# GNN layer pair on one Trainium2 core: the edge loop's accumulators filled by ScalarE, its bias folded into a constant, its attributes scaled before they are turned, and the second LayerNorm's moments taken another way

## The chip, the cores and the metric

One Trainium2 chip, one NeuronCore of it. The metric is the device time of one execution in microseconds (us): the median of three runs of the kernel before is 1620.67 us (1620.6 to 1627.65).

## What is computed

There are N = 50,000 nodes with 128 features and E = 25,000 edges sorted by their receiver `dst`. Cut to what matters:

```python
h = maximum(layernorm(x), 0)
# layer 0, on edges (src, dst):
m = concat([h[dst], h[src]]) @ W_pre.T + b_pre
agg = concat([max, min, mean, std of m over the edges of a node])
scaled = concat([agg, agg * log(deg + 1), agg / log(deg + 1)])
x = x + (concat([h, scaled]) @ W_post.T + b_post) @ W_lin.T + b_lin
h = maximum(layernorm(x), 0)
# layer 1:
mean_attr = segment_mean(edge_attr, dst)
x = x + relu(concat([h, mean_attr]) @ W1 + b1) @ W2 + b2
```

## The kernel before

**Two passes.** The node pass treats every node as if it had no edge, in 98 chunks of 512 nodes. It writes the output rows `y` and a `table` that holds, for every node, its first normalised row and its `x`. The edge pass goes over the edges in 49 chunks of 512 edges (4 tiles of 128). It gathers the sender's and the receiver's rows from `table`, and scatters finished rows over those of the node pass for nodes that have edges. Chunk by chunk each engine runs its own hand-written program; `run_passes` calls `node_step` and then `edge_step` on each of them, and semaphores tie the programs together.

**One edge step.** In step k the engines work on several chunks at once, each in the order that its `edge_step` spells out:

- GpSimd (POOL) gathers the rows of chunk k+4: eight indirect DMAs in `gather`, for four tiles two each. Between them `receiver_const` adds a constant to the receivers' x of chunk k+1 into `xdc`. Then come the four indirect DMAs of `scatter` for chunk k-2, and `mean_attr`, which multiplies the running sum of the attributes by 1/count into `attr_mean` for chunk k.
- TensorE (PE) turns the sender's rows (`turn_sender`) and the receiver's (`turn_receiver`) of chunk k+1, makes the sender's part of the message (`sender_part`), and does the heavy part, `layer0`, in four tiles of chunk k: max, min and mean of the messages, each split into a high and a low part, the deviation and the receiver's row against the combined weights, added up in banks 5 and 6 in turn. For chunk k-1 it turns the second normalised rows (`turn_normed`), computes `hidden` from them and from `attr_mean`, and `outputs`, where one matmul of ones (L701) puts the bias b2 into bank 7 and sixteen add the product.
- ScalarE (ACT) moves turned rows out of PSUM, adds the bias b_pre to the message (`message`), squares it, makes high parts, normalises chunk k-1, and takes roots.
- VectorE (DVE) runs five scans over the 512 edges of a chunk (max, min, sum, sum of squares, attributes) that restart at every new receiver, makes low parts, and for each tile of `layer0` runs `mix`: three operations that scale and add the three 128-column blocks, giving x after layer 0. `moments` takes mean and variance of that from four bn_stats and four bn_aggr. `factors` turns them into scale and shift.
- SyncE (SP) loads masks for chunk k+4 (four rows, broadcast to all partitions) and attributes for chunk k+2.

The gathered rows lie in four buffers, `attr_mean`, `xdc`, `x1` and most others in two. Before a tile of `layer0`, PE waits until `mix` has read that bank (L605); `hidden` waits for POOL's product:

```python
pe.wait_ge(sem("e_attr_mean"), c + 1 + EU * i)
```

The order of PE in a step is turn_sender(k+1), layer0(k,0), sender_part(k+1), turn_receiver(k+1), layer0(k,1), turn_normed(k-1), layer0(k,2), turn_attr(k), hidden(k-1), layer0(k,3), outputs(k-1) (L708 to L730).

## Time and profile before

| | |
|---|---|
| median of three runs | 1620.67 us (1620.6 to 1627.65) |
| the profiled execution, its own time | 1626.46 us |
| its span, first to last instruction | 1624.7 us |
| granted TensorE clock, mean | 0.973 |
| node pass, about | 0 to 560 us |
| edge pass, about | 560 us to the end |
| busy: PE, DVE, POOL, ACT | 1494.9, 1397.1, 1236.0, 939.8 us |
| DMA moved | 197.95 MB, mean 122 GB/s |

A busy engine is one that has an instruction running; an engine's idle time is put down to what ended it. "Issue" stands for time in which nothing that the profile shows was waited for. PE's granted clock is 1.00 at 2.4 GHz and 0.50 at 1.2 GHz. A step of the edge pass is most easily read off a line that runs once per chunk.

### The profile page before, as it was taken

To read this page: it belongs to the slowest core of one execution; us is meant where nothing else is said; L and a number is where in the kernel's file an instruction comes from. 1 tells how busy PE (TensorE), PEld (TensorE's weight loads), DVE (VectorE), ACT (ScalarE), POOL (GpSimd) and SP (SyncE) were. 2 spreads that over 40 slices of the span, in tenths; PEclk is the share of its full clock that TensorE was granted. 3 is DMA by queue.
4 is the path that set the end of the run, shared out by engine and by line. 5 is a ranking of instruction groups with operands and counts; after the bars stand their busy time and mean duration, and the time that the engine had idled before them with its cause. 6 is when DMAs were issued, how large, how long until landed. Compare 5 with 4: busy or idle time off the path is not lost.

```text
span 1624.7 us, 33700 instructions
## 1 busy us (share of the span) xinstructions
PE 1494.9 (92%) x8747; PEld 1257.4 (77%) x8747; DVE 1397.1 (86%) x4327; ACT 939.8 (58%) x1976; POOL 1236.0 (76%) x1376
## 2 busy tenths in 40 slices
PE   2899999999999759999999999999998999999995
PEld 2799998889999648888777787777777777777783
DVE  5899999999999468899888997988887888888892
ACT  1799999999999534455444453434444444444341
POOL 1778777777778777888888888888888888888833
PEclk9899999999999979999999999999999999999997
DMA  3455555555555622233233333333332323333200
GB/s 88 163 209 206 207 207 201 201 201 204 204 203 206 187 87 85 84 86 90 90 91 92 93 92 91 92 91 89 93 91 79 95 86 89 94 93 93 89 18 15
DMA packets 158898, 197.95 MB, mean 122 GB/s; under 512 B 18912, under 2 KB 115321, under 8 KB 158858
## 3 DMA queue, kind: packets, MB, share of 16 engines
q1 hardware_dynamic: 136906, 149.93, 28.3%
q0 software_dynamic: 21952, 47.55, 9.5%
q8 instruction: 17, 0.28, 0.1%
q14 instruction: 23, 0.19, 0.0%
HBM read 111.11 MB, written 90.17 MB: 124 GB/s over the span
## 4 chain that ended last, share of the span: by engine, by line
PE 82%; DVE 6%; issue 5%; ACT 3%; another core or an unknown queue 3%; DMA 1%; SPq 1%; POOL 0%; DVEq 0%; ACTq 0%; POOLq 0%
PE bank L572 12%; PE bank L621 6%; PE bank L581 6%; PE bank L614 5%; PE bank L691 5%; PE bank L618 5%; PE bank L615 5%; PE bank L624 5%; PE bank L704 5%; PE bank L670 3%; PE bank L593 3%; PE bank L591 3%; PE bank L592 3%; PE bank L555 3%
## 5 line engine op out<-in xcount | busy, mean ns | idle before, releaser
L444 POOL DMA_INDIRECT rows<-table,idx x196 | 208.3, 1063 | 59.7 <-issue 59.7
L450 POOL DMA_INDIRECT y<-nout,oidx x196 | 200.0, 1020 | 70.6 <-issue 70.3
L444 POOL DMA_INDIRECT hs<-table,idx x196 | 204.8, 1045 | 44.7 <-issue 31.2
L614 PE MATMUL bank<-comb_lo,agg_hi 128*128 128x384 f32 x588 | 212.4, 361 | 16.6 <-DVE nout L1019 10.7
L572 PE MATMUL bank<-w_sb,nut 128*128 128x128 f32 x1568 | 202.9, 283 | 5.5 <-issue 4.7
L379 POOL TENSOR_TENSOR runs<-nx,b_all 128x512 f32<-128x512 f32 x98 | 125.9, 1284 | 107.9 <-DVE nx L1029 107.8
L572 PEld LDWEIGHTS bank<-w_sb,nut 128*128 128x128 f32 x1568 | 184.5, 193 | 23.1 <-issue 14.2
L618 PE MATMUL bank<-comb_hi,agg_lo 128*128 128x384 f32 x588 | 200.1, 340 | 0.0
L615 PE MATMUL bank<-comb_hi,agg_hi 128*128 128x384 f32 x588 | 199.5, 339 | 0.0
L781 ACT ACTIVATE nh<-nx,nms,nrs 128x128 f32<-128x128 f32 x392 | 161.8, 484 | 1.1 <-DVE nms L1002 0.5
L621 PE MATMUL bank<-comb_sd,agg_sd 128*128 128x384 f32 x392 | 159.6, 489 | 0.0
L865 ACT ACTIVATE nut<-bank,b_col 128x512 f32<-128x512 f32 x98 | 67.5, 689 | 151.9 <-PE bank L696 138.4
L391 POOL TENSOR_SCALAR rows<-rows,nmv,nrs 128x128 f32<-128x128 f32 x196 | 154.6, 798 | 0.0
L388 POOL TENSOR_TENSOR xdc<-rows,lone_const 128x512 f32<-128x512 f32 x98 | 125.1, 1276 | 32.7 <-DVE nrs L1039 32.7
L691 PE MATMUL bank<-attr_mean,w_attr 128*128 128x512 f32 x196 | 111.3, 652 | 30.9 <-issue 30.2
L796 ACT ACTIVATE nut<-bank,b_col 128x512 f32<-128x512 f32 x196 | 125.6, 681 | 15.3 <-remote 11.2
L1100 DVE SCALAR_TENSOR_TENSOR part<-bank,amp_att,xdc 128x128 f32<-128x128 f32 x196 | 67.6, 345 | 75.8 <-remote 27.1
L614 PEld LDWEIGHTS bank<-comb_lo,agg_hi 128*128 128x128 f32 x588 | 111.3, 189 | 20.5 <-issue 14.8
L624 PE MATMUL bank<-comb_h_lo,hdt 128*128 128x384 f32 x196 | 125.0, 638 | 0.0
L810 ACT ACTIVATE hst<-bank 128x512 f32<-128x512 f32 x49 | 29.3, 598 | 164.2 <-PE bank L637 130.5
L615 PEld LDWEIGHTS bank<-comb_hi,agg_hi 128*128 128x128 f32 x588 | 111.6, 190 | 2.2
L618 PEld LDWEIGHTS bank<-comb_hi,agg_lo 128*128 128x128 f32 x588 | 111.1, 189 | 0.0
(180 smaller groups left out, 4196.9 us busy)
## 6 DMA issues: line engine op xcount, KB each, us to landing
table<-rows SPq DMA_DIRECT2D x98, 512.0 KB, 2.7
rows<-in_x SPq DMA_DIRECT2D x98, 256.0 KB, 3.1
y<-nout SPq DMA_DIRECT2D x98, 256.0 KB
inv<-inv_row SPq DMA_DIRECT2D x49, 256.0 KB
attr<-in_edge_attr SPq DMA_DIRECT2D x48, 256.0 KB
keep<-keep_row SPq DMA_DIRECT2D x49, 128.0 KB
reset<-reset_row SPq DMA_DIRECT2D x49, 128.0 KB
lift<-lift_row SPq DMA_DIRECT2D x49, 128.0 KB
```

What stands on the lines that cost most here:

```text
L379: pool.tensor_tensor(nx1b[:, c % 4], nx1[:, c % 2], b2_all[:], ALU.add).then_inc(sem("n_x1b"), 1)
L391: last = pool.tensor_scalar(nh[:, c % 4, j, :], nx[:, c % 4, j, :], nmv1[:, c % 4, j, 0:1], nrs1[:, c % 4, j:j + 1], ALU.subtract, ALU.mult)
L444: pool.indirect_dma_start(out=to[:, s, j, :], out_offset=None, in_=of, in_offset=bass.IndirectOffsetOnAxis(ap=idx[:, s, which, j:j + 1], a ...
L450: pool.indirect_dma_start(out=out, out_offset=bass.IndirectOffsetOnAxis(ap=oidx[:, c % 4, j:j + 1], axis=0), in_=eout[:, c % 2, j, :], in_ ...
L572: mm = pe.matmul(bank[5][:, j * P:(j + 1) * P], nut[:, c % 2, m, j * P:(j + 1) * P], w2_sb[:, m, :], start=(m == 0), stop=(m == 1))
L614: pe.matmul(acc[:, 0:SCALERS * P], hi, w_lo, start=(a == MX), stop=False, skip_group_check=True)
L615: pe.matmul(acc[:, 0:SCALERS * P], hi, w_hi, start=False, stop=False, skip_group_check=True)
L618: pe.matmul(acc[:, 0:SCALERS * P], lo, w_hi, start=False, stop=False, skip_group_check=True)
L621: pe.matmul(acc[:, 0:SCALERS * P], agg_sd[:, c % 2, cols], comb_sd[:].rearrange("p s f -> p (s f)"), start=False, stop=False, skip_group_c ...
L624: mm = pe.matmul(acc[:, 0:SCALERS * P], h[:, c % 2, cols], w[:].rearrange("p s f -> p (s f)"), start=False, stop=(w is comb_h_hi and h is ...
L691: pe.matmul(bank[b][:], w1_attr[:, cols], attr_mean[:, c % 2, :], start=True, stop=False)
L781: last = act.activation(nh2[:, b, j, :], nx1[:, b, j, :], ACT.Identity, scale=nrs2[:, b, j:j + 1], bias=nms2[:, b, j:j + 1])
```

## The change

- **Fills.** ScalarE's new `seed` copies a constant of 384 columns (`acc_seed`) into bank 5 or 6 ahead of every tile of `layer0`; the matmuls add to it, and PE now waits for `e_seeded`. The constant holds b_lin and b_post (which `edge_const` added to the receivers' x before) and what b_pre contributes. `out_bias` copies b2 into bank 7, in place of the matmul of ones. POOL's `receiver_const` goes; `mix` reads the gathered x itself.
- **Bias as a constant.** `message` goes: the scans read the banks 3 and 4, in which `sender_part` now writes in turn, and the square is taken without bias.
- **Attributes scaled, then turned.** ScalarE's `scale_attr` multiplies the rows of attributes by 1/count before PE turns them, and the scan uses a new fp32 mask `keepm` = (count-1)/count, so its result is the mean already. POOL's `mean_attr` goes. `keepm` is one more broadcast row for SP, 256 KB per chunk.
- **Moments.** The third operation of `mix` also puts out the sum of its 128 columns (`accum_out`), `negative_mean` scales it, and ScalarE's `squares` puts out the sum of squares of x minus its mean.
- **Order.** PE's `turn_attr`, `turn_receiver` and `sender_part` move ahead of `layer0(k,0)`; DVE's scans are set in another order; gathers run three chunks ahead and not four, since their buffer is now free only when `mix` has read it.

The diff, cut to its core:

```diff
@@ inputs and setup
+    keepm_row = nc.dram_tensor("keepm_row", [ROWS * RW], F32, kind="Internal").ap()
-    edge_const = sb("edge_const", [P, TILES, P])
+    edge_const = sb("edge_const", [P, P])
+    acc_seed = sb("acc_seed", [P, SCALERS * P])
+    b_pre_wide = sb("b_pre_wide", [P, P])
-    attr_mean = sb("attr_mean", [P, 2, CHUNK])
+    keepm = sb("keepm", [P, 4, CHUNK])
...
+            dve.scalar_tensor_tensor(keepm_sb[R], count[R], -1.0, inv_count[R], ALU.add, ALU.mult).then_inc(sem("masks_done"), 1)
...
+            dve.tensor_tensor(acc_seed[:, 0:P], bank[6][:, P:2 * P], edge_const[:], ALU.add)
+            dve.tensor_copy(acc_seed[:, P:SCALERS * P], bank[6][:, 2 * P:(1 + SCALERS) * P]).then_inc(sem("seed_ready"), 1)
@@ SyncE, edge_step
-                        sp.wait_ge(sem("e_attr_mean"), c - 3 + EU * i)
+                        sp.wait_ge(sem("e_max"), c - 3 + EU * i)
...
+                        sp.wait_ge(sem("e_attr_run"), c - 3 + EU * i)
...
-                    for dst_sb, row in ((keep, keep_row), (reset, reset_row), (lift, lift_row), (inv, inv_row)):
+                    for dst_sb, row in ((keep, keep_row), (reset, reset_row), (lift, lift_row), (inv, inv_row),
+                                        (keepm, keepm_row)):
@@ GpSimd
-            def receiver_const(c, i):
...
-                pool.tensor_tensor(xdc[:, c % 2], xd[:, c % 4], edge_const[:], ALU.add).then_inc(sem("e_xdc"), 1)
...
-                    pool.wait_ge(sem("e_xdc"), c - 3 + EU * i)
+                    pool.wait_ge(sem("e_mixed"), TILES * (c - 3) + TILES * EU * i)
...
-            def mean_attr(c, i):
...
-                pool.tensor_tensor(attr_mean[:, c % 2, :], run_attr[:, c % 2, :], inv[:, c % 4, :],
-                                   ALU.mult).then_inc(sem("e_attr_mean"), 1)
...
             def edge_step(k, i):
-                if edge(k + 1):
-                    copy_scales(k + 1, i)
-                if edge(k + 4):
-                    gather_rows_of(k + 4, i)
-                    pool.wait_ge(sem("e_idx"), k + 5 + EU * i)
-                    go()
-                    gather(k + 4, (0, 1))
-                if edge(k + 1):
-                    receiver_const(k + 1, i)
-                if edge(k + 4):
-                    if edge(k + 1):
-                        pool.wait_ge(sem("e_xdc"), k + 2 + EU * i)
-                        go()
-                    gather(k + 4, (2, 3))
+                if edge(k + 3):
+                    gather_rows_of(k + 3, i)
+                    pool.wait_ge(sem("e_idx"), k + 4 + EU * i)
+                    go(0)
+                    gather(k + 3, (0, 1))
+                if edge(k + 2):
+                    copy_factors(k + 2, i)
+                if edge(k + 3):
+                    if edge(k + 2):
+                        pool.wait_ge(sem("e_factors"), k + 3 + EU * i)
+                        go(1)
+                    gather(k + 3, (2, 3))
                 if edge(k - 2):
...
                     scatter(k - 2)
-                if edge(k):
-                    mean_attr(k, i)
@@ TensorE
             def layer0(c, j, i):
                 acc = bank[5 + j % 2]
...
-                if j >= 2:
-                    pe.wait_ge(sem("e_mixed"), TILES * c + j - 1 + TILES * EU * i)
...
+                pe.wait_ge(sem("e_seeded"), TILES * c + j + 1 + TILES * EU * i)
...
-                    pe.matmul(acc[:, 0:SCALERS * P], hi, w_lo, start=(a == MX), stop=False, skip_group_check=True)
+                    pe.matmul(acc[:, 0:SCALERS * P], hi, w_lo, start=False, stop=False, skip_group_check=True)
...
             def sender_part(c, i):
                 pe.wait_ge(sem("e_hst"), c + 1 + EU * i)
...
-                pe.matmul(bank[3][:], ws_t[:], hst[:, c % 2, :], start=True, stop=True).then_inc(sem("e_b_psum"), 1)
+                pe.matmul(bank[3 + c % 2][:], ws_t[:], hst[:, c % 2, :], start=True, stop=True).then_inc(sem("e_b_psum"), 1)
...
-                    pe.matmul(bank[b][:], w1_attr[:, cols], attr_mean[:, c % 2, :], start=True, stop=False)
+                pe.matmul(bank[b][:], w1_attr[:, cols], run_attr[:, c % 2, :], start=True, stop=False)
...
             def outputs(c, i):
                 pe.wait_ge(sem("e_ut"), 2 * (c + 1) + 2 * EU * i)
-                pe.matmul(bank[7][:], ones[:], b2_rows[:], start=True, stop=False, skip_group_check=True)
+                pe.wait_ge(sem("e_b2"), c + 1 + EU * i)
@@ ScalarE
+            def squares(c, i):
...
+                for j in range(TILES):
+                    last = act.activation(off2[:, j, :], x1[:, b, j, :], ACT.Square, bias=neg2[:, b, j:j + 1],
+                                          accum_out=sq2[:, b, j:j + 1])
...
-            def message(c, i):
...
-                act.activation(bank[4][:], bank[3][:], ACT.Identity, bias=b_pre_col[:]).then_inc(sem("e_b"), 1)
...
-                act.activation(bsq[:, c % 2, :], bank[3][:], ACT.Square, bias=b_pre_col[:]).then_inc(sem("e_bsq"), 1)
+                act.activation(bsq[:, c % 2, :], bank[3 + c % 2][:], ACT.Square).then_inc(sem("e_bsq"), 1)
...
+            def seed(c, j, i):
...
+                act.activation(bank[5 + j % 2][:, 0:SCALERS * P], acc_seed[:], ACT.Copy).then_inc(sem("e_seeded"), 1)
+
+            def scale_attr(c, i):
...
+                for j in range(TILES):
+                    last = act.activation(attr[:, c % 2, j, :], attr[:, c % 2, j, :], ACT.Copy,
+                                          scale=factor[:, c % 4, 2, j:j + 1])
...
+            def out_bias(c, i):
...
+                act.activation(bank[7][:], b2_all[:].rearrange("p j f -> p (j f)"), ACT.Copy).then_inc(sem("e_b2"), 1)
@@ VectorE
-                dve.tensor_tensor(x1[:, c % 2, j, :], acc[:, 0:P], part2[:, j % 2, :], ALU.add).then_inc(sem("e_mixed"), 1)
+                dve.scalar_tensor_tensor(x1[:, c % 2, j, :], acc[:, 0:P], 1.0, part2[:, j % 2, :], ALU.mult, ALU.add,
+                                         accum_out=sum2[:, c % 2, j:j + 1]).then_inc(sem("e_mixed"), 1)
...
-                dve.tensor_tensor_scan(run_attr[:, b, :], keep[:, s, :], bank[2][:], run_attr[:, 1 - b, end] if c else 0.0,
+                dve.tensor_tensor_scan(run_attr[:, b, :], keepm[:, s, :], bank[2][:], run_attr[:, 1 - b, end] if c else 0.0,
...
-            def moments(c, i):
...
-                for j in range(TILES):
-                    last = dve.bn_stats(bn2[:, b, j, :], x1[:, b, j, :])
...
+            def negative_mean(c, i):
...
+                dve.tensor_scalar(neg2[:, b, :], sum2[:, b, :], -1.0 / P, None, ALU.mult).then_inc(sem("e_neg2"), 1)
...
             def edge_step(k, i):
...
                 if edge(k - 2):
                     outputs(k - 2, i)
+                if have:
+                    scan_attr(k, i)
+                if ahead:
+                    scan_min(k + 1, i)
                 if behind:
                     factors(k - 1, i)
                 if have:
                     mix(k, 0, i)
                 if ahead:
+                    receiver_low(k + 1, i)
                     scan_max(k + 1, i)
-                    scan_min(k + 1, i)
-                    scan_sum(k + 1, i)
-                    message_mean(k + 1, i)
-                    receiver_low(k + 1, i)
...
```

What moves on an engine, as the lists of each engine's instructions in program order have it. ScalarE first, one whole step of the edge pass of the kernel before (line, operation, output<-inputs, shape):

```order
L810 ACTIVATE hst<-bank 128x512
L802 ACTIVATE sd<-mv,eps_col 128x4
L835 ACTIVATE bank<-bank,b_pre_col 128x512
L816 ACTIVATE hdt<-bank 128x512
L824 ACTIVATE nh<-nx,ms,rs 128x128 x4
L841 ACTIVATE bsq<-bank,b_pre_col 128x512
L847 ACTIVATE nh2t<-bank 128x512
L853 ACTIVATE agg_hi<-runs 128x512 x2
L859 ACTIVATE mean_b<-mean_b 128x512
L853 ACTIVATE agg_hi<-mean_b 128x512
L865 ACTIVATE nut<-bank,b_col 128x512 x2
L869 ACTIVATE var<-var 128x512
```

and the first twelve rows of the same step with the change; eight rows follow to the step's end, among them one more fill of a tile (L875) and the fill of bank 7 (L888):

```order
L820 ACTIVATE hst<-bank 128x512
L804 ACTIVATE off,sq<-nx,neg 128x128 x4
L842 ACTIVATE bsq<-bank 128x512
L875 ACTIVATE bank<-acc_seed 128x384
L812 ACTIVATE sd<-sq,eps_col 128x4
L826 ACTIVATE hdt<-bank 128x512
L834 ACTIVATE nh<-nx,ms,rs 128x128 x4
L875 ACTIVATE bank<-acc_seed 128x384
L854 ACTIVATE agg_hi<-runs 128x512
L848 ACTIVATE nh2t<-bank 128x512
L882 ACTIVATE attr<-attr,factor 128x128 x4
L875 ACTIVATE bank<-acc_seed 128x384
```

The four squares (L804), whose input DVE finishes last in the step before, now stand ahead of the squared message (L842) and of the fill of tile 1 (L875). The bias copy L835 is gone.

TensorE, around the border between two steps, before:

```order
L624 MATMUL bank<-comb_h_hi,hdt 128x384
L701 MATMUL bank<-b_rows,ones 128x512
L704 MATMUL bank<-w_sb,nut 128x128 x8
L637 MATMUL bank<-ident,hs 128x128 x4
L614 MATMUL bank<-comb_lo,agg_hi 128x384
L615 MATMUL bank<-comb_hi,agg_hi 128x384
```

and with the change:

```order
L607 MATMUL bank<-comb_h_hi,hdt 128x384
L701 MATMUL bank<-w_sb,nut 128x128 x8
L629 MATMUL bank<-ident,hs 128x128 x4
L653 MATMUL bank<-ident,attr 128x128 x4
L643 MATMUL bank<-ident,rows 128x128 x4
L664 MATMUL bank<-hst,ws_t 128x512
L597 MATMUL bank<-comb_lo,agg_hi 128x384
```

The matmul of ones is gone, and three pieces (the turns of the attributes and of the receivers, and the sender's part L664) stand between the sender's turn and the first tile of `layer0`, where none stood.

## Rows read from the trace of the kernel before

**Rows 1.** The page, part 1: busy us (share of the span) xinstructions.
```profile
PE 1494.9 (92%) x8747; PEld 1257.4 (77%) x8747; DVE 1397.1 (86%) x4327; ACT 939.8 (58%) x1976; POOL 1236.0 (76%) x1376
```

**Rows 2.** One line of the code, L701, once per step, in two stretches: first and last start.
```profile
L701 PE MATMUL bank<-b_rows,ones x8: 490/490/498, 645.6 to 780.1; 64*128 64x512 f32 x8
...
L701 PE MATMUL bank<-b_rows,ones x38: 490/490/498, 780.1 to 1556.8; 64*128 64x512 f32 x38
...
L701 PE MATMUL bank<-b_rows,ones x4: 490/490/500, 1556.8 to 1607.0; 64*128 64x512 f32 x4
```

**Rows 3.** Windows: PE, PEld, DVE, ACT, POOL busy (x), granted clock, DMA share, GB/s.
```profile
650.00:780.00 130.00, 130.00 (x678) 106.19 (x676) 120.78 (x242) 66.39 (x125) 107.28 (x127) 1.00 0.31 91
800.00:1540.00 740.00, 693.92 (x3555) 560.23 (x3554) 631.56 (x1313) 332.54 (x631) 604.65 (x700) 0.98 0.31 90
```

**Rows 4.** POOL's groups, 800 to 1540: xcount | busy us, mean ns | idle before, releaser.
```profile
L444 POOL DMA_INDIRECT rows<-table,idx x138 | 149.4, 1083 | 42.1 <-issue 42.1
L444 POOL DMA_INDIRECT hs<-table,idx x138 | 146.3, 1060 | 31.0 <-issue 21.0
L450 POOL DMA_INDIRECT y<-nout,oidx x144 | 145.6, 1011 | 53.1 <-issue 52.7 <-PE bank L696 0.3
L461 POOL TENSOR_TENSOR attr_mean<-runs,inv 128x512 f32<-128x512 f32 x36 | 46.6, 1295 | 0.4
L406 POOL TENSOR_TENSOR xdc<-rows,edge_const 128x512 f32<-128x512 f32 x35 | 45.2, 1292 | 0.6
```

**Rows 5.** Timeline of PE, start us, us, what [idle before]: the wait for attr_mean.
```profile
1147.22 1.23 PE L691 MATMUL bank<-attr_mean,w_attr 128*128 128x512 f32 x2 [2.05 <-issue]
...
1149.53 1.91 PE L691 MATMUL bank<-attr_mean,w_attr 128*128 128x512 f32 x2
```

**Rows 6.** Windows again: the stretch behind that wait.
```profile
1148.20:1151.40 3.20, 3.20 (x7) 1.84 (x6) 3.10 (x5) 0.69 (x1) 2.66 (x4) 0.50 0.53 134
```

**Rows 7.** Timeline of PE: the bias matmul and the one behind it.
```profile
1154.93 0.49 PE L701 MATMUL bank<-b_rows,ones 64*128 64x512 f32 x1
1155.36 0.38 PE L704 MATMUL bank<-w_sb,nut 128*128 128x128 f32 x1
```

**Rows 8.** Timeline: the turn of the sender's rows, and ScalarE behind it.
```profile
705.39 0.60 PE L637 MATMUL bank<-ident,hs 128*128 128x128 f32 x4
...
706.03 0.60 ACT L810 ACTIVATE hst<-bank 128x512 f32<-128x512 f32 x1 [3.63 <-PE bank L637]
```

**Rows 9.** Groups of ACT instructions, by shape, 650 to 780 us.
```profile
L824 ACT ACTIVATE nh<-nx,ms,rs 128x128 f32<-128x128 f32 x28 | 11.5, 487 | 0.0
L835 ACT ACTIVATE bank<-bank,b_pre_col 128x512 f32<-128x512 f32 x7 | 4.6, 662 | 12.8 <-PE bank L670 8.4 <-issue 4.4
L810 ACT ACTIVATE hst<-bank 128x512 f32<-128x512 f32 x6 | 3.6, 598 | 20.2 <-PE bank L637 14.6 <-issue 5.7
L802 ACT ACTIVATE sd<-mv,eps_col 128x4 f32<-128x4 f32 x7 | 2.1, 296 | 5.5 <-issue 3.8 <-DVE mv L1256 1.6
```

**Rows 10.** Timeline, DVE and POOL: a chunk's statistics; a small operation beside POOL's multiply.
```profile
705.37 0.87 DVE L1250 BATCH_NORM_STATS2 bn<-nx 128x6 f32<-128x128 f32 x4
...
706.28 0.18 DVE L1256 BATCH_NORM_AGGREGATE mv<-bn 128x2 f32<-128x6 f32 x1
...
706.38 0.28 DVE L1256 BATCH_NORM_AGGREGATE mv<-bn 128x2 f32<-128x6 f32 x3
...
707.35 1.78 DVE L1144 SCALAR_TENSOR_TENSOR ms<-mv,rs 128x4 f32<-128x4 f32 x1
...
707.80 1.30 POOL L461 TENSOR_TENSOR attr_mean<-runs,inv 128x512 f32<-128x512 f32 x1
```

**Rows 11.** Groups of DVE instructions, by shape, 650 to 780 us.
```profile
L1106 DVE SCALAR_TENSOR_TENSOR part<-bank,amp_att,part 128x128 f32<-128x128 f32 x26 | 9.1, 351 | 0.9
L1115 DVE TENSOR_TENSOR nx<-bank,part 128x128 f32<-128x128 f32 x26 | 7.6, 292 | 0.9
L1142 DVE RECIPROCAL rs<-sd 128x4 f32<-128x4 f32 x7 | 1.2, 172 | 0.1
```

More of the change, by code:

```diff
@@ L538, in _ @@
             pe.wait_ge(sem("count_ready"), 1)
+            pe.matmul(bank[6][:, P:(1 + SCALERS) * P], b_pre_wide[:], part_sum[:].rearrange("p s f -> p (s f)"),
+                      start=True, stop=True)
             for s in range(SCALERS):
@@ L626, in layer0, with open_sums @@
                 mm.then_inc(sem("e_layer0"), 1)
+            def open_sums():
+                pe.wait_ge(sem("n_out"), NODE_CHUNKS)
+                pe.wait_ge(sem("n_ut"), 2 * NODE_CHUNKS)
+                for acc in (bank[5], bank[6]):
+                    mm = pe.matmul(acc[:, 0:SCALERS * P], ident[:], comb_sd[:].rearrange("p s f -> p (s f)"),
+                                   start=True, stop=True, skip_group_check=True)
+                mm.then_inc(sem("e_sums_open"), 1)
             def turn_sender(c, i):
@@ L676, in turn_normed @@
                     pe.wait_ge(sem("e_h2l"), c + EU * i)
+                if not last:
+                    pe.wait_ge(sem("e_hst"), c + 3 + EU * i)
                 for j in range(TILES):
@@ L712, in edge_step @@
                 if have:
+                    turn_attr(k, i)
+                if ahead:
+                    turn_receiver(k + 1, i)
+                    sender_part(k + 1, i)
+                if have:
                     pe.wait_ge(sem("e_hdl"), k + 1 + EU * i)
                     layer0(k, 0, i)
-                if ahead:
-                    sender_part(k + 1, i)
-                    turn_receiver(k + 1, i)
-                if have:
                     layer0(k, 1, i)
@@ L875, in edge_step @@
             def edge_step(k, i):
-                ahead, behind = edge(k + 1), edge(k - 1)
+                have, ahead, behind = edge(k), edge(k + 1), edge(k - 1)
+                if k == 0:
+                    seed(0, 0, i)
                 if ahead:
@@ L879, in edge_step @@
                 if behind:
+                    squares(k - 1, i)
+                if ahead:
+                    message_squared(k + 1, i)
+                if have:
+                    seed(k, 1, i)
+                if behind:
                     spread(k - 1, i)
                 if ahead:
-                    message(k + 1, i)
                     receiver_turned(k + 1, i)
@@ L898, in edge_step @@
                 if ahead:
+                    mean_squared(k + 1, i)
+                if behind:
+                    out_bias(k - 1, i)
+                if ahead:
+                    high_part(ME, "e_mean_b", mean_b[:], k + 1, i)
+                    variance_pos(k + 1, i)
+                    if k >= 0:
+                        seed(k + 1, 0, i)
                     deviation(k + 1, i)
@@ L1262, in edge_step @@
                     outputs(k - 2, i)
+                if have:
+                    scan_attr(k, i)
+                if ahead:
+                    scan_min(k + 1, i)
                 if behind:
@@ L1281, in edge_step @@
                 if have:
[L1282 to L1286 removed]
                     mix(k, 2, i)
+                    mix(k, 3, i)
+                    negative_mean(k, i)
                 if ahead:
                     low_part(ME, mean_b[:], k + 1, i)
[L1290 to L1292 removed]
+                    low_part(MN, run_min[:, (k + 1) % 2, :], k + 1, i)
             run_passes(dve, node_step, edge_step, first_step=-1)
```

222 lines of the change are left out of this document (109 added, 113 removed).

## Prediction

> **What bounds the kernel now.** I read the page first: PE is busy 92% of the span, DVE 86%, POOL 76% [rows 1]. These are averages, so the next view is a clock for the steps. L701 runs once per step of the edge pass. From 645.6 to 780.1 us its eight starts stand 134.5 / 7 = 19.21 us apart; from 780.1 to 1556.8 us its 38 starts stand 776.7 / 37 = 20.99 us apart [rows 2]. The same program has two speeds. The windows tell why: in 650 to 780 us PE is busy 130.00 of 130 us, in 800 to 1540 us only 693.92 of 740, while POOL is busy 604.65 [rows 3].
>
> POOL's idle time has to be read with its cause. Its groups in the second stretch [rows 4] wait for no engine: behind each indirect DMA stands some 0.3 us of "issue". The 420 DMAs took 441.3 us and 126.2 us of idle time before them (0.3 of it a real wait), together 567.5 us, and the stretch holds 740 / 20.99 = 35.3 steps, so 16.1 us per step for the twelve DMAs. The two tensor operations L461 and L406 took 91.8 us, 2.6 us per step. Idle and busy together fill POOL's step. So POOL's own program takes 21 us per step and PE's 19.2. At first PE lives on gathers that were issued four chunks ahead; when that lead is used up, POOL sets the pace. PE then waits for the product `attr_mean`: 2.05 us of "issue" ahead of L691, and the two L691 behind it take 1.91 us instead of 1.23 [rows 5], since the granted clock there is 0.50, its lower level of 1.2 GHz [rows 6]. The wait costs, and the clock that falls behind it costs again.
>
> **The change part by part.** All of it lies in the 49 edge steps; 44 of them lie between 645.6 and 1556.8 us, 911.2 us in all, a mean of 20.71 [rows 2].
>
> POOL loses L461 and L406. Its step becomes 21.0 - 2.6 = 18.4 us. The copy of factors takes 12 columns and not 8, nothing that shows. Its gathers now wait for the last `mix` of chunk k-1 and run three chunks ahead. A gather issued within the first 11 us of step k is needed at the start of step k+2, so over 20 us of lead remain. POOL is hidden if PE's step is over 18.4 us, and nearly so if it is not.
>
> PE loses L701: L704 starts 0.43 us behind it [rows 7]. Its own step becomes 19.21 - 0.43 = **18.78 us**. The other matmuls are as many and as long (the fills replace only a start flag). With POOL out of its way, PE is late nowhere for `attr_mean`, and the clock has no such idle time to fall behind.
>
> Two new waits stand on PE's path. First, `sender_part` comes 1.32 us after the sender's turn starts (three turns of 0.44), and needs `hst`: ScalarE starts 0.64 us after the turn and takes 0.60, ready at 1.24 [rows 8, 9]. A weight load waits with it, so between 0 and 0.25 us; I take 0.15. Second, each tile of `layer0` needs its fill. I lay out one step from the start of the sender's turn. PE: tile 0 at 2.3 us, tile 1 at 5.1, turn_normed at 7.9, tile 2 at 8.3, hidden at 11.1, tile 3 at 14.2, outputs at 17.0, end at 18.9.
>
> ScalarE: `hst` to 1.3; four squares; the squared message; the fill of tile 1. Four ScalarE operations of 128 columns with two column operands take 11.5 / 28 = 0.41 us each in a row [rows 9]. What the output of a sum adds, no row shows: nothing at least, and at most a small instruction of its own as L802, 0.30 us [rows 9]. I take 0.2. Squares end at 1.3 + 4 x 0.6 = 3.7, the squared message at 4.3, a fill takes 0.30 (L802, 4 columns) to 0.60 (L810, 512 columns) [rows 9], by its 384 columns 0.5: done at 4.8, before 5.1. Then DVE's factors at 5.6, tile 0 mixed at about 7.2, normalise done at 7.6, the fill of tile 2 at 8.1, before 8.3. The other fills have over 2 us. The margins of 0.2 to 0.3 us are thin, and with the upper price of 0.30 the first is used up; I charge 0.15 us per step, between 0 and 0.6.
>
> ScalarE's sum per step in the first stretch is 66.39 / 6.77 steps = 9.8 us [rows 3]. Less L835 (0.66), plus squares 2.4, scaled attributes 4 x 0.41 = 1.6, fills 4 x 0.5 = 2.0, bank 7 by L810 0.6: 15.8 us of 19. It fits, at 83%.
>
> DVE's sum is 120.78 / 6.77 = 17.8 us [rows 3]. The statistics go: 0.87 + 0.18 + 0.28 [rows 10], 1.3 us. The third operation of `mix` becomes one like L1106, 351 ns against 292 for L1115 [rows 11], 0.24 us for four; its sum output costs from nothing to L1142's 0.17 [rows 11], I take 0.08 each; `negative_mean` 0.17. DVE also gets time back: L1144 over four columns took 1.78 us while POOL's L461 ran [rows 10], and POOL has no such operation left. I leave that out of the sum. DVE ends near 17.0 us of 19, so it hides. `scan_min` starts at 4.4 and not at the step's start, an idle time of about 1 us, which just fits.
>
> The new mask row is 256 KB in 19 us where the DMA engines were busy 0.31 [rows 3]: hidden by three steps of lead.
>
> **A rule against the change.** Four 128-column ScalarE operations in a row cost 0.41 us each here, one alone 0.487 [rows 9]: part of the fixed cost overlaps. The Trainium skill, VectorE: DVE Perf Modes, section on the TRN2 errata, says that operations of VectorE and ScalarE that read SBUF pay a fixed extra time per instruction, so that many small tiles pay it each time; the change adds thirteen ScalarE instructions that read SBUF. By that rule without overlap the eight small ones would cost 0.49 us each, 0.6 more per step, half of it ahead of tile 1, and the sum would be some 10 us worse.
>
> **The sum.** Step: 18.78 + 0.15 + 0.15 = 19.08 us. 44 steps: 839.5 us against 911.2, -71.7. The step before them and the three behind them (1556.8 to 1607.0 [rows 2]) lose L701 only: 4 x 0.43 = -1.7. The node pass is the same code. The end of the last chunk has a longer way to its root (squares 2.4 us where statistics took 1.3): about +1, and setup as much less or more. Together -73. The profiled execution goes from 1626.46 to about 1553; its time lies 5.8 us over the median of the three runs, and kept at that distance the forecast is **1547 us**.
>
> **The rivals.**
> - *ScalarE is late.* The fills stand in ScalarE's queue behind the squares. If square and sum together take 0.8 us each, the fill of tile 1 is ready at 5.6, and at 0.9 each at 6.0, and that of tile 2 slips too: 0.6 to 1.2 us per step, a step of 19.6 to 20.2, 1570 to 1596 us. For it: margins of 0.2. Against it: ScalarE waited for others most of the time [rows 9]. Chance 0.17.
> - *POOL still sets the pace.* If its DMAs grow (a DMA's mean of 1060 ns over the 0.95 of an undisturbed one is contention), to a step of 20, the lead of about 20 us is used up halfway, and the time is near 1570. For it: 18.4 is close to 18.8. Against it: 2.6 us of its own work and the tensor operations' collisions go. Chance 0.06.
> - *Slower than before.* The same queue with another price: from 1.1 us for a square with its sum, 0.5 above the value taken, the squares end at 5.7, the squared message at 6.3, the fill at 6.8, 1.7 us late, and the fill of tile 2, which waits behind a root, factors and normalise in the same chain, is late by the same and a little more: steps of 20.8, where the gain is gone; at 1.2 us each they are 21.2, and 44 x 0.5 - 2 gives 1641 us. No row of ScalarE shows so dear a small operation. Chance 0.05.
> - *It does not do what it says.* If it is the arrival of the gathers that holds PE and not POOL's program, only L701 counts: 49 x 0.43 = 21 us, or with the new waits against it nothing: 1600 to 1620. Against it: PE's idle time lay ahead of L691, which reads no gathered row [rows 5]. Chance 0.06.
>
> **How the numbers follow.** The forecast has the remaining 0.66. Its own range goes from no new waits (18.78: 1533) to 0.25 + 0.6 (19.63: 1571), with 3 us for the change of passes. The range of 8 in 10 goes from 1531 to 1592: it takes in POOL and most of late ScalarE. A measurement can tell about 0.5% (8 us) from no change. Faster by more: 0.66 + 0.17 + 0.06 and half of the last, less a little for what I have not seen: 0.89. Within: 0.05. Slower: 0.06.
>
> **What would show it.** Right: a line once per step, such as the first output matmul, 19.0 to 19.2 us apart from 620 to 1550 us without a second speed; PE busy over 98% there, the granted clock 1.00 between; POOL waiting for DVE's `mix` once per step; ScalarE near 16 us per step. Wrong: idle time of PE ahead of the tiles of `layer0`, ended by ScalarE's fills (late ScalarE); POOL without waits for another engine and steps that grow later in the pass (POOL); gathers as releasers of the sender's turn.

## The result, and the profile after

| | before | after |
|---|---|---|
| median (runs) | 1620.63 us (1619.68 to 1627.65, 4) | 1747.45 us (1729.56 to 1748.88, 4) |
| span of the profiled execution | 1624.7 us | 1745.6 us |
| granted clock, mean | 0.973 | 0.946 |

The ratio is 1.0747, with a 95% interval of 1.0671 to 1.0823: 7.5% slower, where 1547 us and a range of 1531 to 1592 were forecast. The first thing to say about this number is that it belongs to one of two conditions in which the chips were found. The same changed kernel, not a character altered, took 1519.04 us in a later set of runs (ratio 0.9318, 0.93 to 0.9336) and 1923 us in a third. How this came out, and what tells the conditions apart, is the main part of what follows.

The page of the kernel after, its first part (as [rows 1] of before):

```profile
span 1745.6 us, 34704 instructions
## 1 busy us (share of the span) xinstructions
PE 1510.0 (87%) x8704; PEld 1269.6 (73%) x8704; DVE 1292.3 (74%) x4128; ACT 1137.0 (65%) x2760; POOL 1085.3 (62%) x1280
```

No engine is near its limit any more; every one of them is less busy than the 92% that PE had. The window that answers to the second row of [rows 3] says the same of the edge pass:

```profile
800.00:1540.00 740.00, 633.25 (x3132) 511.11 (x3131) 494.92 (x1033) 423.02 (x1064) 440.64 (x565) 0.94 0.31 92
```

POOL did get its relief: 440.64 us against 604.65. DVE has 494.92 against 631.56. PE, which was to be busy throughout, has 633.25 of 740. So something holds them all. The waits of the edge pass, 800 to 1600 us (us in total, times, longest):

```profile
ACT nh2t L848 <- remote: 191.4, 33, 8.0
POOL idx L439 <- DVE nx L1155: 189.6, 33, 9.5
PEld bank L689 <- issue: 114.7, 34, 5.6
PE bank L689 <- issue: 104.1, 34, 5.2
DVE part L1139 <- remote: 67.6, 18, 5.0
```

The trace calls tiles by the first name of their buffer: `nh2t` at L848 is the edge pass's `h2t`, `nx` at L1155 its `x1`. PE waits 3.1 us per step ahead of L689, the first matmul of `hidden`, which needs `h2t`. ScalarE copies `h2t` at L848 and waits for it 5.8 us per step, for a releaser that the trace cannot name: "remote" stands where no signal of this core's engines is found. Of the two signals that L848 waits for, one is that of PE's `turn_normed` (L674) and the other, of `hidden` two chunks back, is long there. Here is that hand-over in one step, ScalarE's timeline and PE's (start, duration, in brackets the idle time before):

```profile
1204.57 0.60 PE L674 MATMUL bank<-ident,nh 128*128 128x128 f32 x4
...
1207.58 0.33 PE L607 MATMUL bank<-comb_h_hi,hdt 128*128 128x384 f32 x1
1209.46 1.12 PE L689 MATMUL bank<-runs,w_attr 128*128 128x512 f32 x2 [1.54 <-issue]
```

```profile
1208.66 0.60 ACT L848 ACTIVATE nh2t<-bank 128x512 fp32r<-128x512 f32 x1 [4.37 <-remote]
...
1215.93 1.26 ACT L866 ACTIVATE nut<-bank,b_col 128x512 f32<-128x512 f32 x2 [4.58 <-remote]
```

The turn is over at 1205.17 by its record; ScalarE starts 3.5 us later. In all 49 steps the median of this delay is 5.0 us. The second ScalarE line shows the same of `hidden`: its two halves end 1.56 us apart on PE (1211.27 and 1212.83), but ScalarE's two L866 follow each other without a gap. The semaphores' own records in the trace say why. The turn's increment is recorded at 1208.64, and those of `hidden` at 1215.91 and 1215.98. So it is the signals that are late, not (or not only) the work. "Remote" here means a signal that came too long after its matmul to be matched with it. The signals of this stretch arrive in the order of their matmuls: 2.5 us late for tile 1 of `layer0`, 3.5 for the turn, 6.6 for tile 2, 4.6 and 3.2 for `hidden`, 0.5 for tile 3. That is how a queue that fills and drains would look; which one, no trace here shows.

Records are missing as well: of 6027 semaphore increments by instructions of the repeated lines, 787 have none in this trace. The DMAs' increments fare worse: 8,244 are recorded, and 19,116 in a later trace of the same kernel.

### The profile page after: what moved, and what is told of

It reads as the page before. It is cut to its first block, busy times and chain, and to the rows that moved or that the text cites. A ratio compares the mean times of both kernels' runs of the same rounds, so it can differ in the third digit from the quotient of the medians.

```text
span 1745.6 us, 34704 instructions
## 1 busy us (share of the span) xinstructions
PE 1510.0 (87%) x8704; PEld 1269.6 (73%) x8704; DVE 1292.3 (74%) x4128; ACT 1137.0 (65%) x2760; POOL 1085.3 (62%) x1280
## 4 chain that ended last, share of the span: by engine, by line
PE 78%; issue 10%; another core or an unknown queue 4%; ACT 3%; DVE 3%; DMA 1%; SPq 0%; POOL 0%; ACTq 0%; DVEq 0%; POOLq 0%
PE bank L563 11%; PE bank L689 7%; PE bank L604 6%; PE bank L572 5%; PE bank L701 5%; PE bank L597 5%; PE bank L601 5%; PE bank L598 5%; PE bank L607 5%; PE bank L582 3%; PE bank L584 3%; PE bank L583 3%; PE bank L546 2%; PE bank L554 2%
## 5 line engine op out<-in xcount | busy, mean ns | idle before, releaser
L451 POOL DMA_INDIRECT y<-nout,oidx x196 | 214.7, 1095 | 72.3 <-issue 72.3
L689 PE MATMUL bank<-runs,w_attr 128*128 128x512 f32 x196 | 138.3, 796 | 123.4 <-issue 123.4
L445 POOL DMA_INDIRECT rows<-table,idx x196 | 186.7, 952 | 60.2 <-issue 60.2
L597 PE MATMUL bank<-comb_lo,agg_hi 128*128 128x384 f32 x588 | 221.6, 377 | 0.9 <-issue 0.9
L445 POOL DMA_INDIRECT hs<-table,idx x196 | 191.0, 975 | 44.4 <-issue 31.8
L439 POOL COPY idx<-index 128x8 int32 (+1 forms) x49 | 30.6, 624 | 268.0 <-DVE nx L1155 268.0
L1139 DVE SCALAR_TENSOR_TENSOR part<-bank,factor,rows 128x128 f32<-128x128 f32 x196 | 68.3, 348 | 173.2 <-remote 79.7
L848 ACT ACTIVATE nh2t<-bank 128x512 fp32r<-128x512 f32 x49 | 29.3, 597 | 248.1 <-remote 234.8
L866 ACT ACTIVATE nut<-bank,b_col 128x512 f32<-128x512 f32 x98 | 64.7, 686 | 140.3 <-PE bank L693 87.2
L689 PEld LDWEIGHTS bank<-runs,w_attr 128*128 128x128 f32 x196 | 43.4, 242 | 144.1 <-issue 136.9
L597 PEld LDWEIGHTS bank<-comb_lo,agg_hi 128*128 128x128 f32 x588 | 111.5, 190 | 15.1 <-issue 12.7
```

Source lines behind the costliest of these rows:

```text
L445: pool.indirect_dma_start(out=to[:, s, j, :], out_offset=None, in_=of, in_offset=bass.IndirectOffsetOnAxis(ap=idx[:, s, which, j:j + 1], a ...
L451: pool.indirect_dma_start(out=out, out_offset=bass.IndirectOffsetOnAxis(ap=oidx[:, c % 4, j:j + 1], axis=0), in_=eout[:, c % 2, j, :], in_ ...
L597: pe.matmul(acc[:, 0:SCALERS * P], hi, w_lo, start=False, stop=False, skip_group_check=True)
L689: pe.matmul(bank[b][:], w1_attr[:, cols], run_attr[:, c % 2, :], start=True, stop=False)
```

## The experiments

I call a set of runs *quiet* when its traces lack next to no semaphore update by an engine's instruction (1 to 7 of some 6000) and *disturbed* when they lack hundreds. "h2t delay" is the start of L848 (or its line in that kernel) less the recorded end of the turn, the median over the stretch of the line shown. The step is measured on the same line, once per chunk.

**Four edits in one set.** The rivals for the late signals were PE's own sequencer (A), transfers (D) and the fills of PSUM (F).

```diff
@@ x1_filler: TensorE, between layer0(k, 2) and hidden
+                if behind and have:
+                    if k >= 2:
+                        pe.wait_ge(sem("e_out"), k - 1 + EU * i)
+                    for _ in range(14):
+                        pe.transpose(bank[7][:, 0:P], ident[:], ident[:])
@@ x2_nomasks: SyncE; the scans wait for 80, once
-                if edge(c):
+                if edge(c) and c < 4:
@@ x3_nogather: GpSimd; PE and DVE wait for the first gathers alone
-                if edge(k + 3):
+                if edge(k + 3) and k + 3 < 4:
@@ x4_noseed: ScalarE's four fills gone, layer0 waits for e_mixed as before
-                    pe.matmul(acc[:, 0:SCALERS * P], hi, w_lo, start=False, stop=False, skip_group_check=True)
+                    pe.matmul(acc[:, 0:SCALERS * P], hi, w_lo, start=(a == MX), stop=False, skip_group_check=True)
```

> The changed kernel with 14 useless 128-column turns (about 0.11 us each, 1.5 us a step, 48 steps) put on TensorE between the third tile of layer0 and hidden, into bank 7, which hidden's first matmul overwrites; the computation is whole. What is to be explained: in the changed kernel ScalarE copies h2t some 5 us after the turn of the normed rows has ended by its record, TensorE's first matmul of hidden waits 3.1 us a step, and its signals come late. Theory A (TensorE's signals come late while its sequencer stands in front of hidden): the sequencer passes on to the useless work, stands shorter, the delay shrinks from 5 us to under 2, and the time falls or stays, 1640 to 1740, in spite of 73 us of added work. Theory D (transfers in flight delay the signals): the delay stays near 5 us, the filler only fills the idle time: 1735 to 1770. Theory F (the fills of banks 5 and 6 by ScalarE): as D. If the step were simply full of work, 1747 + 73 = 1820.

> The changed kernel, but the five mask rows are loaded for the first four chunks alone and used again (the output is wrong from the fifth chunk on; SyncE's 0.9 MB of broadcasts per step are gone, the rows of attributes are still loaded). Theory D in the form that the burst of broadcasts, which fills the DMA engines just as the normed rows are turned, delays TensorE's signals: the delay of h2t goes from 5 us to under 1, and the time to 1560 to 1600. Theory A: without effect on the waits of the sequencer, delay 4 to 5 us, 1730 to 1750. Theory F: 1730 to 1750.

> The changed kernel, but rows are gathered for the first four chunks alone and used again (wrong output; eight indirect DMAs of GpSimd per step are gone, the four scatters and all broadcasts stay). Theory D in the form that GpSimd's indirect DMAs delay TensorE's signals: the delay of h2t under 1 us (no scatter is issued at that time), the time 1560 to 1620. Theory D with the broadcasts as the cause: delay 3 to 5 us, 1680 to 1750. Theories A and F: 1720 to 1750.

> The changed kernel without ScalarE's fills of banks 5 and 6: each tile of layer0 starts its own sum, as before, and the constant is left out (wrong output). Theory F (ScalarE writing PSUM beside TensorE's sums, or its longer queue, is what delays): the delay of h2t falls to under 1 us and the time to 1540 to 1600. Theories A and D: the delay stays 4 to 5 us, and the time at 1725 to 1750.

Measured: 1590.13, 1518.21, 1519.01 and 1514.11 us, beside 1629.03 for the kernel before. The three without added work lie 26 to 42 us under the lowest value expected of any theory, and the filler 50 us under it, useless work included. Four unlike edits with one effect are suspect: a control was missing.

**The control, and smaller doses.** c4_nokeepm loads the new mask row for four chunks alone.

> The changed kernel with no edit, as a control. Four different small edits each gave about 1515 us or, with 73 us of useless work added, 1590 us, where the changed kernel had 1747 us. Theory K (the kernel has two modes and sits close to the border: any small relief or shift tips it into the good one): again 1730 to 1750 us. Theory S (the session or the chip made the difference, not the edits): about 1515 us, like the others.

> The changed kernel with 2 useless turns (0.2 us) per step between the third tile and hidden; computation whole. Theory K with a threshold in the work behind the turn of the normed rows: 1700 to 1750 if 0.2 us is not enough, about 1520 if it is. Theory S: 1515 + 48 x 0.22 = 1526.

> The same with 6 useless turns (0.65 us). Theory K: somewhere between 2 and 14 turns the good mode begins; if here, 1515 + 48 x 0.65 = 1546, else 1700 to 1750. Theory S: 1546.

> The changed kernel with the new mask row keepm loaded for the first four chunks alone (wrong output from the fifth on); the other four rows are loaded as before the change. Theory K with the load on the DMA engines as the part that matters: 256 KB of 1.15 MB less per step gives the good mode, about 1515 us. Theory K with another part: 1700 to 1750. Theory S: 1515.

Measured: 1519.04 (1518.1 to 1520.05, 4 runs; ratio 0.9318, 0.93 to 0.9336), 1529.02, 1549.66 and 1519.27 us. The unedited kernel is as fast as its edited forms: theory S stands, K falls, and the first four runs say nothing about the late signals. They say something about the quiet condition, though. With 0, 2, 6 and 14 useless turns the time is 1519.0, 1529.0, 1549.7 and 1590.1: (1590.1 - 1519.0) / (14 x 48) = 0.106 us per turn, paid in full. PE sets the end there, and gathers, masks and fills are hidden. The control's window and its L848 line, 640 to 1420 us:

```profile
800.00:1400.00 600.00, 600.00 (x3244) 507.60 (x3244) 507.96 (x1071) 439.77 (x1105) 487.03 (x583) 1.00 0.39 116
```

```profile
L848 ACT ACTIVATE nh2t<-bank x42: 598/600/601, 643.8 to 1404.5; 128x512 fp32r<-128x512 f32 x42
its engine sat idle before it (us, times) until:
  PE bank L674: 37.0, 42
```

PE busy 600 of 600 us at clock 1.00; steps of (1404.5 - 643.8) / 41 = 18.55 us; ScalarE waits 0.9 us per step, with PE's turn as a named releaser.

**Both kernels again, and a test of the first step of the prediction.** p1_nomean is the kernel before without POOL's `mean_attr`; the waits of SyncE and DVE for `e_attr_mean`, not shown here, go over to signals of the scans and of `hidden`.

```diff
@@ GpSimd, edge_step
-                if edge(k):
-                    mean_attr(k, i)
@@ TensorE, hidden
-                pe.wait_ge(sem("e_attr_mean"), c + 1 + EU * i)
+                pe.wait_ge(sem("e_attr_run"), c + 1 + EU * i)
```

> The kernel before the change with no edit, to have its trace beside that of the control. In the first session (whose traces of before and after were read above) 846 and 787 semaphore updates are missing from the traces and TensorE's signals come late; in the control's trace 2 are missing and none is late. Theory S1 (the first session was disturbed, and that touched the kernel before too): 1627 to 1633 us here; no late signals, h2t copied within 0.15 us of the turn throughout; POOL still sets the pace from about 780 us on, with steps near 21 us. Theory S2 (the kernel before has late signals everywhere): delays of 1.5 to 2.7 us in its second half, as in the first session.

> The changed kernel with no edit once more, in a session of its own. Theory S: 1515 to 1522 us if the session is like the last two; 1730 to 1750 us, with TensorE's signals late, if it is like the first. Theory K has fallen with the control.

> The kernel before without GpSimd's mean_attr: hidden takes the running sums as they are (wrong output), nothing else changes; GpSimd loses one tensor operation of about 1.3 us per step. If GpSimd's own program sets the pace from 780 us on, as the prediction has it, the 38 steps there shrink by 1.3 us each, 49 us, to 1575 to 1590 us. If something else sets it (the arrival of the gathers, TensorE itself), 1620 to 1633 us.

Measured: 1616.47 us (1603.56 and 1629.37), 1923.31 us (ratio 1.1876, 1.1776 to 1.1976) and 1566.96 us (ratio 0.9676, 0.9561 to 0.9791). This set was disturbed (800, 721 and 915 updates missing), on the very chip that had given the quiet set of the first four edits: it is not a property of a chip. The changed kernel lies 173 us above the upper end that was expected of a disturbed set, so "disturbed" is not one level. The kernel before has the late signals too, with a median of 1.7 us from 811 to 1511 us, so S1's "no late signals" is wrong and S2 right; but they cost it nothing that its time shows: 1618.33 us in this set, 1631.02 in the control's. p1 confirms that POOL set the pace: one tensor operation less, and from 640 to 1480 us its steps are 19.3 us apart, with PE busy 595.69 of 600. It lies 8 us under its range, since PE is then nearly free of POOL over the whole pass. And p1, PE-bound in a disturbed set, has an h2t delay of 0.04 us. Late signals are not everywhere. Nor is a gather in flight enough. In one of p1's steps the turn ended at 1038.76 and ScalarE copied `h2t` at 1038.81, while POOL was in the middle of its gathers:

```profile
1033.35 0.95 POOL L448 DMA_INDIRECT rows<-table,idx  x1 [0.30 <-issue]
1034.33 1.29 POOL L410 TENSOR_TENSOR xdc<-rows,edge_const 128x512 f32<-128x512 f32 x1
...
1036.03 0.97 POOL L448 DMA_INDIRECT hs<-table,idx  x1
1037.30 0.95 POOL L448 DMA_INDIRECT rows<-table,idx  x1 [0.30 <-issue]
1038.56 0.95 POOL L448 DMA_INDIRECT hs<-table,idx  x1 [0.30 <-issue]
```

```profile
1038.81 0.60 ACT L849 ACTIVATE nh2t<-bank 128x512 fp32r<-128x512 f32 x1 [0.17 <-issue]
```

Here a tensor operation parts the eight gathers into two fours. The signal of `turn_attr`, one tile of `layer0` further on, is late in p1, by 1.2 us at the median.

**What makes the signals late.** The same edits, now beside their own control.

> The changed kernel with no edit, as the level for the three below. It took 1747 us in the first set of runs, 1519 in the control's and 1923 in the last. Each trace tells the condition of its set by two marks: semaphore updates missing from the trace (2 in the quiet one, 787 and 721 in the others) and h2t copied late (0.04, 5.0 and 8.3 us at the median). 1515 to 1522 us if the set is quiet, 1730 to 1930 if not.

> The changed kernel with 14 useless turns (1.5 us) per step ahead of hidden, whole computation, once more. In a quiet set 1590, as before. In a disturbed one: theory A (TensorE's signals come late because its sequencer stands in front of hidden's wait): the delay shrinks by half or more, and the time is 1600 to 1700. Theory D (transfers delay them, whatever TensorE does): delay as in the unedited kernel, and the time at most 1.5 us per step below it, or equal.

> The changed kernel with the mask rows loaded for four chunks alone (wrong output), once more. Quiet: 1518. Disturbed, theory D by the broadcasts (the DMA engines are full, share 1.0, just while the normed rows are turned): delay under 1 us, 1520 to 1600. Theory D by GpSimd's indirect DMAs, or theory A: delay 4 us or more, 1700 to 1900.

> The changed kernel with rows gathered for four chunks alone (wrong output), once more. Quiet: 1519. Disturbed, theory D by GpSimd's indirect DMAs: delay under 1 us, 1520 to 1600. Theory D by the broadcasts: delay 2 to 5 us, 1620 to 1800. Theory A: 1700 to 1900.

The set was disturbed. The L848 line (L853 with the filler) of each, with the idle time before it, in this order: unedited, filler, no masks, no gathers:

```profile
L848 ACT ACTIVATE nh2t<-bank x39: 597/597/597, 703.0 to 1733.6; 128x512 fp32r<-128x512 f32 x39
its engine sat idle before it (us, times) until:
  remote: 337.3, 38
```

```profile
L853 ACT ACTIVATE nh2t<-bank x37: 597/597/597, 735.0 to 1725.9; 128x512 fp32r<-128x512 f32 x37
its engine sat idle before it (us, times) until:
  remote: 326.4, 36
```

```profile
L848 ACT ACTIVATE nh2t<-bank x43: 597/597/600, 656.7 to 1679.1; 128x512 fp32r<-128x512 f32 x43
its engine sat idle before it (us, times) until:
  remote: 256.8, 43
```

```profile
L848 ACT ACTIVATE nh2t<-bank x43: 597/599/602, 652.6 to 1431.5; 128x512 fp32r<-128x512 f32 x43
its engine sat idle before it (us, times) until:
  PE bank L674: 53.4, 42
```

| kernel | time us | h2t delay us | step us | updates missing |
|---|---|---|---|---|
| unedited | 1899.24 | 8.8 | 27.1 | 734 |
| 14 useless turns | 1927.96 | 8.8 | 27.5 | 706 |
| no masks | 1797.30 | 5.4 | 24.3 | 842 |
| no gathers | 1545.81 | 0.5 | 18.5 | 351 |

Each is one run. Theory A falls: the filler changes the delay by nothing (its time lies 29 us above the unedited kernel's, where D had it equal or below). Theory D holds, and the gathers are the larger part. With them gone the masks and the scatters alone delay by 0.5 us; with the masks gone the gathers and scatters alone delay by 5.4; all together by 8.8. The steps are back at the quiet kernel's 18.5 us as soon as the gathers stop. (The 27 us that this run lies above the quiet 1519 arose before its first step: its first turn ends at 634 us and not at 607.)

**Why the kernel before is spared.** The change took POOL's two tensor operations out from between its DMAs, and altered where gathers lie against `turn_normed`. g1 gives the operations back (`pause` is a product of 128x512 elements into a row that nobody reads), g2 changes the place.

```diff
@@ g1_pauses: GpSimd, behind each gather(k + 3, ...) of edge_step
+                    if k >= 0:
+                        pause()
@@ g2_after_h2t: GpSimd, edge_step: copy_factors, then scatter, then
+                    gather_rows_of(k + 3, i)
+                    if k >= 1:
+                        pool.wait_ge(sem("e_h2t"), k + EU * i)
+                    pool.wait_ge(sem("e_idx"), k + 4 + EU * i)
+                    go(0)
+                    gather(k + 3, (0, 1, 2, 3))
```

> The changed kernel with two useless tensor operations of 512 columns (about 1.3 us each) given back to GpSimd, one behind each four gathers, where the kernel before had receiver_const and, in another place, mean_attr; the computation is whole. GpSimd's own program becomes about 15.1 + 2.6 = 17.7 us per step, under TensorE's 18.5. Theory B (a backlog: eight indirect DMAs one behind the other, with no pause, queue up something behind which TensorE's signals wait; without gathers the delay was 0.5 us, with them 8): in a disturbed set the pauses shrink the delay from 8 us to under 3, and the time from 1900 to 1540 to 1700. Theory D without backlog (a gather in flight delays, whatever lies between): delay 7 to 9 us, 1850 to 1930. Quiet set: 1515 to 1530 by either.

> The changed kernel with GpSimd's order turned: the four scatters of chunk k-2 first, then the eight gathers of chunk k+3 in a row, held until ScalarE has copied h2t; whole computation. No gather is in flight while the normed rows are turned and h2t is waited for. Theories B and D: in a disturbed set h2t's delay falls to under 1.5 us, and the lateness moves to the signals of hidden and of the fourth tile, which stand in the gathers' stretch: the wait of outputs grows; 1600 to 1780 us. If gathers are not what delays the signals: delay 7 to 9 us, 1850 to 1930. Quiet set: 1515 to 1530.

> The kernel of the run before (scatters first, the eight gathers held until h2t is copied; whole computation) once more, since that set was quiet: 4 and 7 semaphore updates missing, 1518 us beside 1519 for the unedited kernel. If this set is disturbed: theories B and D want h2t's delay under 1.5 us and the lateness at hidden's and the fourth tile's signals instead, 1600 to 1780 us; if gathers are not what makes the signals late, the delay stays 7 to 9 us, 1850 to 1930. If it is quiet again: 1515 to 1522 us, and the question of the place stays open.

The first two fell into a quiet set (4 and 7 updates missing): 1572.13 us (ratio 0.9662, 0.9634 to 0.969) and 1518.21 us (0.933, 0.9303 to 0.9357). For g1 both theories had said 1515 to 1530, and that was wrong: POOL's program is 15.1 us busy per step in the control and 3.0 us of "issue" ahead of the DMAs, 18.0 together, and I had left the 3.0 out. Two operations of 1.05 us make it 20.1. From 905.5 to 1513.7 us g1's 31 copies of `h2t` lie 20.3 us apart, and before that 18.5, while the gathers' lead lasted: the picture of [rows 2] again.

The third run met a disturbed set (864 missing): 1672.84 us (ratio 1.0318, 1.0244 to 1.0393). Its L845, as L848 above, and PE's largest wait from 800 to 1400 us:

```profile
L845 ACT ACTIVATE nh2t<-bank x41: 577/599/602, 653.9 to 1518.4; 128x512 fp32r<-128x512 f32 x41
its engine sat idle before it (us, times) until:
  PE bank L671: 33.2, 34
```

```profile
PE bank L661 <- ACT hst L817: 49.1, 22, 3.1
```

The h2t delay is 0.12 us, in a condition that gave 5.0 and 8.8 before. The lateness has moved to the signals that now fall behind the gathers. One is `turn_sender`'s, on which `hst` and so `sender_part` (L661) wait, 1.8 us per step over 28 steps, and the steps are 21.6 us. From 640 to 1520 us those of `outputs` (at the median 2.1 us late), `turn_receiver` (2.0) and `turn_attr` (2.4) are late too. I had expected it at `hidden`'s signals; those are on time. So the place of the gathers decides which hand-over is hit. Whether pauses between them would let the lateness drain (theory B) was not tried in a disturbed set and stays open; p1's parted gathers speak for it, but p1 differs in more than that. No version tried beats both kernels in both conditions. g2 equals the changed kernel in the quiet one and is slower than before in the other. Its 1672.84 us lie under all disturbed runs of the unedited kernel (1747, 1923, 1899), but no unedited kernel ran in that set, so how much of this is g2's is not shown.

## Why the prediction was wrong, and where it was right

**The step that failed** is in "The change part by part": "Its own step becomes 19.21 - 0.43 = 18.78 us", with two waits of 0.15 on top. The sum priced each hand-over from PE to ScalarE at nothing but its own work, and the wait of `hidden` for `h2t`, which is neither of the "two new waits", at nothing. In the set of the result `turn_normed`'s signal came 5.0 us late, and the changed kernel has 2.75 us of matmuls between that turn and `hidden`. A step grew to (1614.6 - 715.8) / 38 = 23.65 us:

```profile
L848 ACT ACTIVATE nh2t<-bank x39: 597/597/598, 715.8 to 1614.6; 128x512 fp32r<-128x512 f32 x39
its engine sat idle before it (us, times) until:
  remote: 219.1, 38
```

The quiet kernel's is 18.55. Of the 5.1 us between them PE's wait at L689 is 104.1 / 34 = 3.1 and the wait at L701 for ScalarE's fill of bank 7, behind the late `hidden`, 10.7 / 34 = 0.3. The other 1.7 is PE itself, busy 633.25 / 740 x 23.65 = 20.2 us per step for the same matmuls, at a clock of 0.94 and not 1.00. Of the 228 us between 1747 and 1519, 208 arise between the first and the last L848 (628.3 to 1721.8 us against 606.8 to 1492.0) and 21 before the first, a part that the forecast took as unchanged.

**The trace of before had the sign.** In its second stretch ScalarE's L847 waits for "remote" 18 times:

```profile
L847 ACT ACTIVATE nh2t<-bank x28: 597/599/602, 954.6 to 1526.7; 128x512 fp32r<-128x512 f32 x28
its engine sat idle before it (us, times) until:
  remote: 40.8, 18
```

The delay is 1.4 to 2.7 us in most of the steps concerned, against 0.04 to 0.6 in the first stretch. It cost the kernel before little. My reading, which no run tests by itself, is that PE stood ahead of L691 for POOL's `attr_mean` at that very place [rows 5]: a wait of its own covered the late one. I read the 2.05 us there as POOL's alone. The change took the cover away, and by taking work out of POOL it moved the eight gathers together around the turn: in the step of 1135 us they start from 7.1 us before its end to 2.1 behind it.

**No rival named it.** "Slower than before" had the right sign and the wrong mechanism. ScalarE was never late by its own queue: a square with its sum took 0.38 us in a row, not 1.1 (in the control four of them ran from 1156.11 to 1157.64). The four rows of attributes took 1.26 us together, 0.32 each. The Trainium skill, VectorE: DVE Perf Modes, in its section on the TRN2 errata, has a fixed extra time per instruction, by which I had reckoned 0.49 each without overlap; in a row these did overlap.

**In the quiet condition,** where nothing stands in the way of the sum, it can be held against each term:

| term | forecast | control |
|---|---|---|
| POOL's program per step | 18.4 | 18.0 |
| PE's step | 19.08 | 18.55 |
| wait for `hst`, for fills | 0.15 + 0.15 | 0, 0 |
| ScalarE busy per step | 15.8 | 13.6 |
| DVE busy per step | 17.0 | 15.7 |
| sum output: ScalarE, DVE | 0.2, 0.08 | 0.19, 0.08 |
| time | 1547 | 1519 |

The two outputs of sums are instructions of their own in the control:

```profile
L804 ACT ACTIVATION_READ_ACCUMULATOR off<-nx,neg 128x1 f32 x12 | 2.3, 191 | 0.0
```

```profile
L1155 DVE DVE_READ_ACCUMULATOR nx<-bank,part 128x1 f32 x13 | 1.1, 83 | 0.0
```

PE's step was mis-sized by 0.5 us, and 44 x 0.5 = 22 of the 28 us follow from that. Of it 0.3 is the two waits that did not come. The other 0.23 is the new order of PE's pieces: from the first matmul of `sender_part` to the next block is 0.54 us in the control, where it was 0.86 between two tiles of `layer0` in the kernel before, and the sixteen output matmuls take 0.10 less; against that the three turns, now in a row, take 0.18 more. The sums of ScalarE and DVE were 2.2 and 1.3 us too high (DVE's terms add to 17.2, not 17.0); both engines are hidden, so nothing hangs on it. So POOL's relief and the second speed's end were read rightly, and even there the time lay below the range, which had no case in which PE's own step came out shorter than 18.78.

## What to carry to other kernels

A kernel that is bound by a slow engine has slack in all its other hand-overs; once that engine is relieved, each of them must be asked how late its signal may be, and a wait whose releaser the profile cannot name is a reason to measure first. Run the unedited kernel in the same set as its experiments: without it four edits looked like four cures. And of two orders that cost the same, the one with more work between a signal and the instruction that needs it back should be the safer; no run here tried that with useful work.

## What was unexpected

- PE's semaphore signals can arrive 5 to 10 us behind the recorded end of the matmul, several then within 0.07 us of each other, around GpSimd's gathers. The kernel with 14 useless turns ran twice on the same chip: once with an h2t delay of 0.04 us and 1590.13 us in all, once with 8.8 and 1927.96.
- The lateness comes with lost records. Each DMA raises its semaphore 16 times; the control's trace has 25,492 updates, 5,784 more than without gathers (45 chunks x 8 DMAs x 16 = 5,760) and 3,592 more than without masks (45 x 5 x 16 = 3,600), and it is these two groups with which the delay shrinks. Every execution here was made with its records being taken, at 25,492 semaphore updates and 34,704 instructions in the control's 1516 us. The Trainium skill, NOTIFIC — the notification-queue block, section 7.1, says that this block's internal pipeline holds its producers up rather than lose a record. By that rule the recording itself could be what holds PE's signals back. The missing records speak against the second half of the rule, or for a loss elsewhere; no run here was made without recording, so whether the 1747 us would be there unobserved is open, as is what makes a set quiet or disturbed.
- An operation with a sum output is two instructions: 0.19 us more on ScalarE, of which half overlaps in a row, and 0.08 us on DVE.
